# Router sums moved up on VectorE, the fourth router weight slot in space of its own

## The reference

```python
x = x + tanh(g_xattn[0]) * xattn(layernorm(x), ctx, mask, Wq, bq, Wk, bk, Wv, bv, Wo, bo)
x = x + tanh(g_ffn[0]) * ffn(layernorm(x), w1, b1, w2, b2, w3, b3, gate_w, gate_b)

# ffn, for each token
gate_weights = softmax(x @ gate_w + gate_b)            # 512 -> 8
topk_vals, topk_idx = top_k(gate_weights, 2)
h = gelu(x @ w1[e] + b1[e]); h = gelu(h @ w2[e] + b2[e]); y_e = h @ w3[e] + b3[e]
out = sum(topk_vals * y_topk)
```

## Time and profile before

| | us |
|---|---|
| median of three runs | 1785.81 |
| the profiled execution | 1788.41 |
| its span | 1786.6 |
| TensorE busy | 1754.9 |
| VectorE busy | 1242.9 |
| ScalarE busy | 953.5 |

### The profile page before, as it was taken

One profiled execution on the slowest core, in us unless ns is written; L12 is line 12 of the kernel. 1 busy time (PEld: TensorE's weight loads), 2 busy tenths in 40 slices (PEclk: granted clock), 3 DMA queues, 4 the chain that ended last, 5 costly groups with the idle time before them and its releaser, 6 DMA issues. The chain is left out here.

```text
span 1786.6 us, 39812 instructions
## 1 busy us (share of the span) xinstructions
PE 1754.9 (98%) x14694; PEld 1518.9 (85%) x14694; DVE 1242.9 (70%) x3382; ACT 953.5 (53%) x1780; POOL 181.3 (10%) x271
## 2 busy tenths in 40 slices
PE   9999999999999999999999999999999999999997
PEld 8887888888888888888888877877899999999996
DVE  5676777777778777777777456556677777777772
ACT  4655655555555556555555535445555555455551
POOL 1111110110011011101100010000000101101110
PEclk9999999999999999999999999999999999999999
DMA  8992231232133222312212489998766666667661
GB/s 264 354 329 68 84 85 54 80 79 78 46 84 86 72 62 84 85 51 83 71 38 94 153 282 395 360 346 312 218 205 211 211 209 217 217 217 217 215 196 36
DMA packets 123229, 292.68 MB, mean 164 GB/s; under 512 B 17859, under 2 KB 36291, under 8 KB 123088
## 3 DMA queue, kind: packets, MB, share of 16 engines
q1 hardware_dynamic: 99664, 225.46, 37.7%
q0 software_dynamic: 23424, 65.30, 13.1%
HBM read 244.04 MB, written 46.66 MB: 163 GB/s over the span
## 5 line engine op out<-in xcount | busy, mean ns | idle before, releaser
L1173 ACT ACTIVATE probs<-probs,neg_max 100x722 f32<-100x722 f32 x248 | 221.0, 892 | 107.2 <-DVE neg_max L1524 107.2
L1517 DVE CUSTOM_DVE_ANT_0 probs<-bank_rows,mask_sb 100x362 f32<-100x362 f32 x496 | 234.5, 529 | 6.7 <-PE bank_rows L761 6.6
L2603 DVE TENSOR_TENSOR w_low<-stage,w_high 128x1024 fp32r<-128x1024 f32 x176 | 213.1, 1222 | 36.0 <-ACT w_high L2507 35.5
L1178 ACT ACTIVATE p_t<-bank_rows 121x600 f32<-121x600 f32 x256 | 171.2, 669 | 76.5 <-PE bank_rows L771 74.5
L2507 ACT ACTIVATE w_high<-stage 128x1024 fp32r<-128x1024 f32 x176 | 183.4, 1056 | 35.3 <-DMA stage<-in_L_ffn_w 35.2
L2359 PE MATMUL bank_rows<-h_low,w_high 128*128 128x256 f32 x704 | 199.2, 283 | 0.0
L2359 PE MATMUL bank_rows<-h_high,w_low 128*128 128x256 f32 x704 | 199.2, 283 | 0.0
L2359 PE MATMUL bank_rows<-h_high,w_high 128*128 128x256 f32 x704 | 199.2, 283 | 0.0
L2530 ACT ACTIVATE gelu<-bank_rows,biases 128x256 f32<-128x256 f32 x176 | 82.1, 472 | 219.4 <-PE bank_rows L2359 195.6
L771 PE MATMUL bank_rows<-ident,probs 100*121 100x100 f32 x1488 | 180.7, 257 | 16.0 <-ACT p_t L1178 15.8
L771 PEld LDWEIGHTS bank_rows<-ident,probs 100*121 100x121 f32 x1488 | 160.3, 156 | 40.9 <-ACT probs L1173 19.4
(11 more groups left out here) (252 smaller groups left out, 3837.1 us busy)
## 6 DMA issues: line engine op xcount, KB each, us to landing
stage<-in_L_ffn_w SPq DMA_DIRECT2D x240, 512.0 KB, 4.7
plain_w<-in_L_ffn_w SPq DMA_DIRECT2D x15, 2048.0 KB, 12.4
expert_in_rows<-filling POOLq DMA_DIRECT2D x8, 3341.0 KB, 15.8
router_rows<-in_gate_rows POOLq DMA_DIRECT2D x84, 200.0 KB, 3.6
ctx_raw<-in_ctx SPq DMA_DIRECT2D x16, 720.0 KB, 4.9
ctx_raw<-in_ctx SPq DMA_DIRECT2D x15, 724.0 KB, 4.4
xs_sb<-expert_in_rows SPq DMA_DIRECT2D x11, 514.0 KB, 5.3
router_rows_last<-in_gate_rows POOLq DMA_DIRECT2D x28, 200.0 KB, 3.4
```

Of the source, the lines that this page charges most:

```text
L1173: nc.scalar.activation(p, p, ACT.Exp, bias=neg_max[:, h:h + 1], scale=-1.0, accum_out=exp_sum[:, h:h + 1]).then_inc(probs_ready, 1)
L1178: nc.scalar.activation(p_t[:, h % HQ, :, :].rearrange("t (k i) s -> t k (i s)", k=2), bank_rows[0:TT, 4:6, 0:3 * S], ACT.Copy).then_inc(pt ...
L1517: nc.vector.tensor_tensor_reduce(out=probs_of(b, g)[:, q, at], in0=score_bank[q][0:S, 0:size], in1=mask_sb[:, at], scale=-1.0, scalar=BIG, ...
L2603: nc.vector.tensor_tensor(lo, src, hi.bitcast(F32), ALU.subtract).then_inc(chunk_lo[which], 1)
```

## The change

`dots` writes its products over `x_res`, so the tile `dot_rows` goes; its place becomes router slot 0, and the fourth slot no longer lies over the fillings' source. All four slots are loaded ahead of the last filling, and the fillings go out at every 5.5 instead of every 6 of the scores' instructions. Since `x_res` is overwritten, `dots` waits until the store of `x_res` to `out` has landed (`x1_stored`), and SyncE loads the next `x_res` only after the eighth sum. On VectorE the sums stand earlier, three in group 1 instead of two, and the reciprocals of group 1 go behind the first half of group 2's scores.

```diff
@@ attention, placing
-    dot_rows = place("dot_rows", [S, D])
+    router_rows = [place("router_rows_0", [S, D])]
...
-    router_rows = [place(f"router_rows_{k}", [S, D]) for k in range(ROUTER_SLOTS - 1)]
-    router_rows.append(nc.alloc_sbuf_tensor_at("router_rows_last", [S, D], F32, offset=filling_at))
+    router_rows += [place(f"router_rows_{k}", [S, D]) for k in range(1, ROUTER_SLOTS)]
@@ on_gpsimd
-            pool.wait_ge(scored, 6 * e + 1)
+            pool.wait_ge(scored, 11 * e // 2 + 1)
             if e == E - 1:
-                for k in range(ROUTER_SLOTS - 1):
+                for k in range(ROUTER_SLOTS):
                     load_router(k)
...
         pool.wait_ge(regions_filled, 16 * E)
-        pool.wait_ge(spare_filled, 32 * TPB)
-        load_router(ROUTER_SLOTS - 1)
@@ on_sync, store_and_load
             store(t)
+            if t < IN_ROWS:
+                sp.wait_ge(router_dot, E * t + E)
             sp.dma_start(x_res[:], batch_rows(x, b)).then_inc(xres_loaded, 16)
@@ on_vector, dots
+            dve.wait_ge(x1_stored, 16 * t + 16)
             for e in es:
...
-                    out=dot_rows[:], in0=x2[:, 0, 0:D], in1=router_rows[k][:], scale=1.0, scalar=0.0,
+                    out=x_res[:], in0=x2[:, 0, 0:D], in1=router_rows[k][:], scale=1.0, scalar=0.0,
@@ on_vector, body
             if odd:
                 queries_low(b, "Q23")
-                dots(t, (0, 1))
+                dots(t, (0, 1, 2))
                 keys_low(b, n, 0, 0)
             else:
                 keys_low(b, n, 0, 0)
-                dots(t, (0, 1))
+                dots(t, (0, 1, 2))
                 keys_low(b, n, 1, 0)
+
+            score(b, 2, 0)
             recips(b, 1)
-
-            score(b, 2, 0)
-            dots(t, (2,))
+            dots(t, (3,))
             keys_low(b, n, 2, 0)
             score(b, 2, 1)
             scale_o(b, b, 1)
-            dots(t, (3, 4))
+            dots(t, (4, 5))
             values_out(b, 1 - odd, 1)
-            dots(t, (5, 6, 7))
+            dots(t, (6, 7))
             biased(t)
```

More of the change, by code:

```diff
@@ L391, in attention @@
     ctx_high_1 = place("ctx_high_1", [P, DT, HALVES[1][1]], F32R)
-    filling_at = shared_from + place.at
     filling = place("filling", [P, 1, ROW])
```

## The result

The changed kernel took 1835.65 us, the median of four runs (1833.78 to 1836.4); the kernel before took 1785.48 beside it. The ratio is 1.0279, with a 95% interval from 1.0261 to 1.0297: 50 us slower, where 41 were forecast, and inside the range.

A forecast was written before the change was run, and what follows sets the result against it. TensorE, busy 1754.9 of 1786.6 us, was taken as the bound. Stalls 39.6 - 11.8 regained + 13.5 clock + 0 for body 1 = +41.3 on 1788.4: 1829.7, expected median 1827 us, range 1804 to 1842.

The forecast's parts named there:

- parts 1 and 5: Attention stage: earlier sums end TensorE's idle at head 11's transposes, gain 11.8 us; later loads and reciprocals cost nothing.
- part 2: Before K20, bodies 2 to 13: VectorE's wait for the store's landing delays `keys_low`, 39.6 us of new TensorE idle.
- part 3: After the new idle times, TensorE's clock falls in nine of twelve bodies, 1.5 us each: 13.5 us.
- part 4: Body 1 and the fillings: K20 3.0 us late, 2.7 idle and 1.5 slow clock gone; between -1.2 and +3.7, taken as 0.
- The rival of the heavier clock: Group 2: clock falls after every stall and costs 12 x 2.0 instead of 13.5 us; +52, 1838 us; chance 0.12.

The follow-up runs named there:

- the two versions without the stall: The changed kernel with the sums' products over `x_ln` instead of `x_res`, 1774.53 us; the changed kernel with the store issued ahead of the second context load, 1774.82 us.

## Why the prediction was right, point by point

**The bound and the attacked wait** (parts 1 and 5): right. 15.8 us became 1.3, the 14.5 us of bodies 1 to 14 (11.8 and 2.7). The late loads of `x_res` and `x_ln` cost nothing, as the version with the store first shows.

**The wait for the store** (part 2): right in place and mechanism, and nearly in size. 39.6 us for twelve bodies were reckoned and 36.6 measured; with body 1, 3.0 reckoned and 4.5 measured, it is 42.6 against 41.1. The odd bodies' range of -0.10 to 0.12 was misread, since in body 9 SyncE passed 0.21 us ahead of K20; that moves the sum by only 0.2 us. The landing that SyncE saw before was the landing that VectorE met. The wait added alone and the two versions without the stall show that it is the whole loss. Body 4 had 3.26 us where 3.55 were reckoned. Here the measurement also decided against the estimate from the Trainium skill (DMA: Bandwidth & Descriptors, on the anatomy of one DMA), by which the twelve stalls would have been 21.6 us where 36.6 were measured.

**The clock** (part 3): right in kind, too small, and the weakest step. Nine falls at 1.5 us, 13.5 us, were taken for bodies 2 to 13. There were twelve, four of them of double length, so 16 stretches of 3.4 us, and TensorE's busy time grew by 22.3 us. The price of a stretch was right, 1.4 us instead of 1.5. The number was not: that a fall can last for two stretches stood in none of the cases. The reason given for a fall did not hold quite either, since three of the odd bodies had less idle time than the 2.7 us of body 1 (2.54, 2.60 and 2.68), and the clock fell there too. The products that keep TensorE busy give 21 us back, and so confirm the term as the clock's.

**Body 1** (part 4): 0 was taken. It had the longest stall, 4.5 us instead of 3.0: the first sum started at 127.4, where the landing was put at 126. The store had gone out at 120.35, so it was 7.0 us to the first sum, not 5.3. The 2.7 us and one slow stretch went, and one slow stretch came, so it cost about 2 us.

**The sum.** Stalls of bodies 2 to 13 36.6, head 11 -11.8, clock 22.3 and body 1's idle time 1.8 give 48.9 us, where 41.3 were forecast and the spans of the two profiled executions differ by 47.8. The stalls of bodies 2 to 13 were reckoned 3.0 us too long and body 1 1.8 us too short, which partly cancels, by luck; the clock is 8.8 us short and makes nearly all of the gap. The medians differ by 50 and not 48, since the profiled execution before lay 2.6 us above its median.

The rival of the heavier clock, with 1838 us, was the nearest to the result: it had a fall after every stall, and that came true. Its 2.0 us for each fall is near the 1.9 measured, but its reason (denser products in group 2) was not tested; what the rows show is 1.4 us for each 3.4 us of slow clock, and four falls of double length.

## What to carry to other kernels

Before a tile is reused as scratch, look at who reads it last, and if that is a DMA, at when it lands: a store that nobody waited for may stand behind a large load that waits for something else, and putting it ahead of that load made the same wait free. An idle time of 2 or 3 us on TensorE has to be priced twice, once for itself and once for the slow stretch behind it, here 1.4 us for each 3.4 us. And the way to see what an edit in several parts is worth is to take each part alone: here one line held the whole loss, the order of the sums the whole gain, and the slots and fillings next to nothing.

## What the runs showed of the hardware that was not expected

- At an idle time of 2.5 to 4.5 us TensorE's clock fell every time in the changed kernel, 13 of 13: nine times for 3.4 us and four times for 6.8. The four are those where it fell 0.7 us or more before TensorE went on. With the wait alone in the kernel before it was the same: three falls at 1.0 to 1.9 us before TensorE went on lasted 6.8 us, one at 4.6 us before lasted 10.2, and the nine that came after it had gone on lasted 3.4.
- With six products in the stall the clock fell after the five idle times from 1.88 to 3.26 us and not after the eight from 1.13 to 1.84. In other kernels it fell after 1.29, 1.57 and 1.78 us, and it stood after 1.27 us in the kernel before. So the kernel before runs near this edge. Its runs spread over 5 to 6 us, and the long ones have the lower clock: in the 22 runs of the kernel before beside the experiments, the six with a granted clock of 0.996 took 1787.3 to 1789.4 us, the seven with 0.998 took 1783.5 to 1787.3. That falls in the attention stage are the cause was not shown: the profiled execution, with 1788.4 us a long one, has just one.
- Twelve 128 x 128 float32 products of the identity that nobody reads, 2.87 us in all, held the clock at its full level through the stall in 12 bodies of 13 and made the kernel 21 us faster.
